# Attention on one core: value products in blocks of four steps, the reciprocal kept in PSUM, second-batch statistics later

## The reference

```python
h = _layernorm(x, axis=-1) * (1 + ca) + sa          # x: (2, 2048, 256)
q = _split_heads(x @ Wq + bq, 16)                   # 16 heads of 64
k = _split_heads(x @ Wk + bk, 16)
v = _split_heads(x @ Wv + bv, 16)
pattern = jnp.einsum('bhid,bhjd->bhij', k, q) * scale
prob = jax.nn.softmax(pattern, axis=-2)
out = jnp.einsum('bhis,bhid->bhsd', prob, v)
x = x + ga * (concat @ Wo + bo)
```

## Time and profile before

| | |
|---|---|
| median of 3 runs | 4973.08 us (4967.43 to 4975.9) |
| the profiled execution | 4973.04 us, its span 4971.3 us |
| mean granted clock of PE | 0.966 of 2.4 GHz |
| PE busy | 4594.8 us, 92% |
| DVE, POOL, ACT busy | 3502.5 us (70%), 2747.1 us (55%), 2208.0 us (44%) |

### The profile page before, as it was taken

How to read it: one execution, slowest core, us unless ns; L and a number is a source line. 1 busy time by engine, 2 the same in 40 slices (tenths; PEclk the granted TensorE clock), 3 DMA queues, 4 the chain that set the end, 5 groups by cost and what they waited for, 6 DMA issues and landing times.

```text
span 4971.3 us, 65114 instructions
## 1 busy us (share of the span) xinstructions
PE 4594.8 (92%) x21552; PEld 2807.0 (56%) x21552; DVE 3502.5 (70%) x4564; ACT 2208.0 (44%) x3535; POOL 2747.1 (55%) x1172
## 2 busy tenths in 40 slices
PE   6999999999999999999999999957989897999898
PEld 5555555555555555555555555425767675767576
DVE  5878778788788888887877878664656444655455
ACT  5434344444443444444444443424655343556442
POOL 2656566656565666566656655715666223666322
PEclk9999999999999999999999999978999998999898
DMA  2000000000000000000000000010000100000001
GB/s 64 1 5 1 5 6 1 6 5 2 6 1 5 5 1 6 5 2 6 1 5 6 1 6 1 2 55 1 1 1 1 36 1 17 1 1 1 0 1 34
DMA packets 56826, 37.55 MB, mean 8 GB/s; under 512 B 32572, under 2 KB 55056, under 8 KB 56464
## 3 DMA queue, kind: packets, MB, share of 16 engines
q1 hardware_dynamic: 56464, 33.02, 2.3%
HBM read 28.54 MB, written 4.19 MB: 7 GB/s over the span
## 4 chain that ended last, share of the span: by engine, by line
POOL 47%; issue 28%; PE 13%; DVE 7%; ACT 4%; POOLq 1%; DMA 0%; DVEq 0%; SPq 0%; ACTq 0%
POOL accp L709 36%; PE psum L1703 4%; POOL lp L731 4%; PE psum L1578 3%; POOL accp L705 3%; POOL rnorm L721 2%; POOL qk_u L726 2%; DVE ssq L1178 1%; ACT lp L894 1%; PE psum L1624 1%; ACT qk_sq L878 1%; PE psum L1716 1%; DVE qk_w L1190 1%; DVE lneg L1204 1%; PE psum L412 1%
## 5 line engine op out<-in xcount | busy, mean ns | idle before, releaser
L709 POOL TENSOR_TENSOR accp<-accp,prob 128x1024 f32<-128x1024 f32 x640 | 1636.8, 2558 | 744.4 <-ACT prob L848 707.2
L848 ACT ACTIVATE prob<-psum 128x1024 f32<-128x1024 f32 x1024 | 1040.1, 1024 | 1632.3 <-PE psum L1429 1505.8
L1076 DVE TENSOR_REDUCE mx<-psum 128x1 f32<-128x512 f32 x1984 | 1273.3, 683 | 419.9 <-PE psum L1400 380.5
L1440 PE MATMUL psum<-prob,vv 128*64 128x512 f32 x4096 | 997.3, 608 | 0.0
L1428 PE MATMUL psum<-qhh,klh 128*128 128x512 f32 x2048 | 840.7, 411 | 39.3 <-issue 20.4
L1429 PE MATMUL psum<-qlm,kh 65*128 65x512 f32 x2048 | 829.2, 405 | 0.0
L1400 PE MATMUL psum<-klh,qhh 128*128 128x512 f32 x1984 | 727.5, 426 | 56.6 <-DVE mx L1076 52.3
L1400 PEld LDWEIGHTS psum<-klh,qhh 128*128 128x128 f32 x1984 | 353.2, 192 | 467.8 <-DVE mx L1076 307.6
L1440 PEld LDWEIGHTS psum<-prob,vv 128*64 128x64 f32 x4096 | 249.6, 136 | 515.0 <-issue 369.8
L1428 PEld LDWEIGHTS psum<-qhh,klh 128*128 128x128 f32 x2048 | 398.7, 195 | 200.1 <-issue 86.2
L1429 PEld LDWEIGHTS psum<-qlm,kh 65*128 65x128 f32 x2048 | 398.7, 195 | 95.0 <-issue 7.6
(11 more groups left out here) (190 smaller groups left out, 6580.3 us busy)
## 6 DMA issues: line engine op xcount, KB each, us to landing
rot_l<-const_rot SPq DMA_DIRECT2D x2, 2048.0 KB, 8.7
out<-lpT SPq DMA_DIRECT2D x32, 128.0 KB, 1.8
wqkv_l<-L_ffn_wqkv SPq DMA_DIRECT2D x4, 768.0 KB, 9.8
w_l<-L_ffn_w SPq DMA_DIRECT2D x4, 682.0 KB
wqk<-L_attn_Wq SPq DMA_DIRECT2D x32, 64.0 KB, 2.2
wqk<-L_attn_Wk SPq DMA_DIRECT2D x32, 64.0 KB, 2.2
wv_p<-L_attn_Wv SPq DMA_DIRECT2D x16, 128.0 KB, 2.3
wo_p<-L_attn_Wo SPq DMA_DIRECT2D x16, 128.0 KB, 2.0
```

Of the source, the lines that this page charges most:

```text
L709: pool.tensor_tensor(acc_p[cp][:], first[:], prob[kt % PRING][:], ALU.add).then_inc(pool_sum, 1)
L848: act.activation(prob[t % PRING][:], psum[:, S_BANK + 2 * (t % 2):S_BANK + 2 * (t % 2) + 2, :].rearrange("p a b -> p (a b)"), ACT.Exp, sca ...
L1076: dve.tensor_reduce(mx4[:, j // CHUNKS, j % CHUNKS:j % CHUNKS + 1], ps, AX_X, ALU.max).then_inc(ring_free, 1)
L1440: mm = pe.matmul(psum[j * DH:(j + 1) * DH, O_BANK, :], vv[:, kt, s * DH:(s + 1) * DH], prob[t % PRING][:, j * T:(j + 1) * T], start=(kt == ...
```

## The change

Four edits:

- **Blocks of four.** `VALUES = 4`: PE's order is scores of four steps with some nine ring tiles spread between them, then the value products of four steps in one block. `PRING` is 8. The ring tiles are redistributed (`max_places`), and one order entry moves: at the head's end the block of steps 28 to 31 stands behind all four `proj_qk` items, where before steps 28 and 29 stood ahead of them.
- **Reciprocal in PSUM.** The reciprocal is written over the SUM's own ring place, and the two multiplications read it there. The place is released behind the multiplications; before it was released behind the reciprocal. Buffer `rcp` goes.
- **Second-batch statistics later.** ACT evicts the first hidden tiles first; means and squares are interleaved with the evictions of `vv` and with the reads of the input.
- **Buffers.** Three quarters of the second batch's input and a scratch tile lie in `prob[4:8]`; ACT's first exponential waits until POOL has normalised them (`h1_ok`).

```diff
-PRING = 4
+PRING = 8
...
-        GROUPS = STEPS // 2
-        SUM0_GROUP = (KT + 5) // 2
+        VALUES = 4
+        GROUPS = STEPS // VALUES
+        SUM0_GROUP = (KT + 5) // VALUES
+        OUT_GROUPS = 2
+        OUT_EACH = WO_ITEMS // OUT_GROUPS
+        TURN_EACH = 2
...
-            weight = [4] * (GROUPS - 1) + [0]
-            weight[0] = 1
-            weight[SUM0_GROUP + 1:SUM0_GROUP + 3] = [0, 2]
+            weight = [8] * (GROUPS - 1) + [4]
+            weight[0] = 6
+            weight[SUM0_GROUP + 1] = 4
...
-                if g + 1 < GROUPS:
-                    order += tiles[:cut0] + [("scores", 2 * g + 2)] + tiles[cut0:cut1] + [("scores", 2 * g + 3)] + tiles[cut1:]
-                else:
+                steps = range(VALUES * (g + 1) - 2, min(VALUES * (g + 2) - 2, STEPS))
+                n = len(steps)
+                for j, t in enumerate(steps):
+                    order.append(("scores", t))
+                    order += tiles[len(tiles) * j // n:len(tiles) * (j + 1) // n]
+                if g + 1 == GROUPS:
+                    if projects:
+                        order += [("proj_qk", i) for i in range(2)]
                     if maxima:
                         order.append(("turn", 0))
                     if projects:
-                        order += [("proj_qk", i) for i in range(QK_ITEMS)]
-                order += [("values", 2 * g), ("values", 2 * g + 1)]
+                        order += [("proj_qk", i) for i in range(2, QK_ITEMS)]
+                order += [("values", VALUES * g + j) for j in range(VALUES)]
...
-            next_statistics(0)
-            next_statistics(1)
             act.wait_ge(su_d, 3)
...
+                (next_squares if i % 2 else next_means)(i // 2)
+            next_means(2)
+            next_squares(2)
             act.wait_ge(gabo_ok, B)
-            for k in range(TWINS):
+            for k in range(2 * TWINS):
                 read_input(k)
...
+            next_means(3)
+            next_squares(3)
...
+            act.wait_ge(h1_ok, QUADS - 1)
...
-                dve.reciprocal(rcp[:], ps).then_inc(ring_free, 1)
-                dve.wait_ge(ring_free, OFF_RING + RING + rb + i + 1)
+                dve.reciprocal(ps, ps).then_inc(rcp_ok, 1)
+                dve.wait_ge(rcp_ok, G * CP + cp + 1)
...
-                                           o_raw[cp][rows, :], rcp[rows, :], ALU.mult)
-                op.then_inc(oT_ready, 1)
+                                           o_raw[cp][rows, :], ps[rows, :], ALU.mult)
+                op.then_inc(ring_free, 1)
+                dve.wait_ge(ring_free, OFF_RING + RING + rb + i + 1)
+                dve.sem_inc(oT_ready, 1)
```

More of the change, by code:

```diff
@@ L181, in adaln_block @@
         st_rs = sb("st_rs", [P, B, KT], at=att)
-        squares = [sb("squares", [P, 2, D], at=att), o_raw[0][:].rearrange("p (t d) -> p t d", d=D)]
+        squares = [prob[7][:, 0:2 * D].rearrange("p (t d) -> p t d", d=D), o_raw[0][:].rearrange("p (t d) -> p t d", d=D)]
         copies = o_raw[1][:].rearrange("p (t d) -> p t d", d=D)
@@ L189, in adaln_block @@
         x_quads = [[quad(t) for t in acc_p + acc_d],
-                   [x_tail[:, 4 * q:4 * q + 4, :] for q in range(3)] + [x_last[:]]]
+                   [quad(t) for t in prob[4:7]] + [x_last[:]]]
         h_quads = [[quad(t) for t in prob], [h_next[:, 4 * q:4 * q + 4, :] for q in range(QUADS)]]
@@ L292, in adaln_block @@
         PH_STORE = PH_L0 + 2 * LAYERS
-        GROUPS = STEPS // 2
-        SUM0_GROUP = (KT + 5) // 2
+        VALUES = 4
[4 more added lines that the diff above has]
+        TURN_EACH = 2
         def max_places(outs):
-            weight = [4] * (GROUPS - 1) + [0]
-            weight[0] = 1
-            weight[SUM0_GROUP + 1:SUM0_GROUP + 3] = [0, 2]
+            weight = [8] * (GROUPS - 1) + [4]
+            weight[0] = 6
+            weight[SUM0_GROUP + 1] = 4
             for g in outs:
-                weight[g] = 3
+                weight[g] = 6
             return [-(-RING_MAX * sum(weight[:g + 1]) // sum(weight)) for g in range(GROUPS)]
         FIRST, MIDDLE, BRIDGE, LAST = 0, 1, 2, 3
-        TURN_GROUP = 1 + WO_ITEMS // 2
+        TURN_GROUP = 1 + OUT_GROUPS
         def head_order(which, hh):
@@ L316, in head_order @@
             maxima, projects = not (last and hh), not last
-            outs = () if which == FIRST or hh else range(1, 1 + WO_ITEMS // 2)
-            turns = range(TURN_GROUP, TURN_GROUP + TWINS) if which == BRIDGE and hh == 0 else ()
+            outs = () if which == FIRST or hh else range(1, 1 + OUT_GROUPS)
+            turns = range(TURN_GROUP, TURN_GROUP + TWINS // TURN_EACH) if which == BRIDGE and hh == 0 else ()
             placed = max_places([*outs, *turns])
@@ L325, in head_order @@
                 if g in outs:
-                    tiles += [("out", 2 * (g - 1)), ("out", 2 * (g - 1) + 1)]
+                    tiles += [("out", OUT_EACH * (g - 1) + j) for j in range(OUT_EACH)]
                 if g in turns:
[L328 to L332, removed]
-                if g + 1 < GROUPS:
-                    order += tiles[:cut0] + [("scores", 2 * g + 2)] + tiles[cut0:cut1] + [("scores", 2 * g + 3)] + tiles[cut1:]
-                else:
+                    tiles += [("turn_h", TURN_EACH * (g - TURN_GROUP) + j) for j in range(TURN_EACH)]
+                steps = range(VALUES * (g + 1) - 2, min(VALUES * (g + 2) - 2, STEPS))
[6 more added lines that the diff above has]
+                        order += [("proj_qk", i) for i in range(2)]
                     if maxima:
@@ L780, in centred_squares, with next_means @@
                     act.activation(squares[b][:, i % 2, :], x_quads[b][q][:, t, :], ACT.Square, bias=st_neg[:, b, i:i + 1], accum_out=st_ssq[:, b, i:i + 1]).then_inc((sq_ok, sq1_ok)[b], 1)
-            def next_statistics(q):
+            def next_means(q):
                 if q == 0:
@@ L789, in next_statistics, with next_squares @@
                     act.activation(copies[:, i % 2, :], x_quads[1][q][:, t, :], ACT.Copy, scale=-1.0 / D, accum_out=st_neg[:, 1, i:i + 1]).then_inc(neg1_ok, 1)
+            def next_squares(q):
                 act.wait_ge(neg1_ok, 4 * (q + 1))
```

2 lines of the change are left out of this document (removed).

## The result

The changed kernel took 5036.32 us (median of 4 runs, 5032.78 to 5037.19) against 4970.26 us before (4 runs): ratio 1.0131, 95% interval 1.0114 to 1.0149. It is **slower by 66 us**, on the forecast's side and inside its range, 48 us above the predicted 4988. The profiled execution has a span of 5035.3 us at a mean granted clock of 0.953 of 2.4 GHz.

The account below looks back on a forecast made before the run. PE's own sequence was taken to bound the heads, so a change counts by what it removes or adds as waits. The terms -87 - 14 + 42 + 55 + 4 + 15 = +15 gave 4988 us, range 4935 to 5045.

Parts of the forecast that it names:

- Part 2, the start: At the start, moving ACT's statistics behind the evictions removes waits of PE and DVE: together -14 us.
- Part 3, the multiplication: In the heads, DVE's multiplication reading PSUM leaves contention with POOL and takes 0.69 us, bounds 0.69 and 2.04.
- contended rival: In the heads, the multiplication stays contended with POOL at 2.04 us: +84, 5072 us; chance 0.12.
- Part 4, the third max tile: Behind the middle SUM, PE waits 1.75 us for the ring place held until the multiplications end: +42 us.
- Part 5, the late add: At the SUM ending a pair's first head, PE waits 7.2 us for the add chain, 15 times: +55 us.
- hidden-add rival: At the SUM, POOL's chain ends before PE arrives, so the late add costs no wait: 4865 us; chance 0.05.
- Part 1, fewer blocks: In 31 heads, 16 value blocks become 8, saving 0.35 us for each of 248 blocks: -87 us.
- Part 6, the clock: Behind the longer waits at head boundaries, PE's clock falls low; 1 us added each: +15 us.
- rival in which the clock goes the other way: In the heads, denser blocks of four recover half the time lost to the low clock: 4943 us; chance 0.2.
- Part 5's last sentence: Behind a pair's second head, the values' projection covers the add chain; only 0.25 us remains each time: +4 us.
- the -60 of the old waits: At head boundaries, PE's old waits for DVE's last projection item and a ring place, 4.0 us 15 times, vanish.
- the -12 at the ring: Behind the middle SUM, DVE's backlog had cost PE some 0.4 us later; this was subtracted, 31 times.

Follow-up runs that it names:

- e6: The changed kernel with the reciprocal written to an SBUF buffer again and the ring place released behind it: 5201.02 us, ratio 1.0446.
- e3: The changed kernel with the group behind the middle SUM given weight 1, so one max tile stands there: 5011.66 us, ratio 1.0042.
- e7: The changed kernel with tile 12's add ahead of the projections in both heads and ring weights 3 (first group), 1 (behind the SUM), 5 (last): 4901.36 us, ratio 0.9845.
- e8: The kernel before, still in blocks of two, with the reciprocal in PSUM and the later second-batch statistics: 4871.79 us, ratio 0.9783.
- e1: The changed kernel with DVE's add of tile 12 ahead of the four projection items in both heads of a pair: 4954.51 us, ratio 0.9914.
- e9: The changed kernel with DVE's fourth tile 11 in place of 12 and the ring tiles spread in another way: 4942.5 us, ratio 0.9925.
- after_again: The changed kernel run once more, unaltered, against the kernel before: 5034.82 us, ratio 1.0114.
- e2: The changed kernel with DVE's add of tile 12 ahead of the projection items in the second head of a pair alone: 5033.67 us, ratio 1.0077.
- e12: The kernel before in blocks of two, with PSUM reciprocal, late statistics and the add of tile 12 behind the projections: 5073.38 us, ratio 1.0186.
- e10: The kernel before in blocks of two, with PSUM reciprocal, late statistics and DVE's fourth tile 11 in place of 12: 4870.88 us, ratio 0.9777.

## Why the prediction was right in direction and 48 us short

**Part 2, the start (-14):** measured -16.8.

**Part 3, the multiplication (0.69 us):** measured 0.686, never contended. The rule of the GPSIMD Engine Reference of the Trainium skill (Specifications), that POOL contends with VectorE instructions that have two SBUF inputs, agrees with both sides: one input in PSUM has one duration, and e6, back in SBUF, has 1565 ns and 157 us more. The trace before separates the cases: 23 of the 128 multiplications ran with POOL idle, and all took 683 to 690 ns; 101 had a POOL add beside them for over half of their time, with a median of 2522. In the change 81 of 128 had one, and none took over 693. The contended rival is out.

**Part 4, the third max tile (1.75 us, +42):** measured 1.53; 31 x (1.53 - 0.4) = +35. e3 removes it and gains 44, so with the low clock behind it this part was right to within a few us.

**Part 5, the late add (7.2 us, +55):** measured 6.97, with each step of the chain within 0.15 us of the walk. 15 x (6.97 + 0.45 - 4.0) = +51. The hidden-add rival is out.

**Part 1, fewer blocks (-87):** what the break costs was right, but it is not net. In the change a block behind a bunch of two max tiles has the break of before, one behind three has more. The timeline has one of each; the sum goes from the first tile of the bunch to the second record behind the block:

```profile
2038.05 0.64 PE L1409 MATMUL psum<-klh,qhh 128*128 128x512 f32 x2
2038.62 3.65 PE L1449 MATMUL psum<-prob,vv 128*64 128x512 f32 x16
2042.20 0.50 PE L1437 MATMUL psum<-qhh,klh 128*128 128x512 f32 x1
2042.54 0.40 PE L1438 MATMUL psum<-qlm,kh 65*128 65x512 f32 x1
...
2057.34 1.01 PE L1409 MATMUL psum<-klh,qhh 128*128 128x512 f32 x3
2058.28 3.65 PE L1449 MATMUL psum<-prob,vv 128*64 128x512 f32 x16
...
2062.20 0.40 PE L1438 MATMUL psum<-qlm,kh 65*128 65x512 f32 x1
```

Behind two tiles it is 4.49 us, where 3 x 0.23 + 8 x 0.43 = 4.13 would do: 0.36. Behind three it is 4.86, where 4.36 would do: 0.50. With 90 blocks behind three and 57 behind two in the heads the mean is 0.45, and the gain 31 x (16 x 0.35 - 8 x 0.45) = -62. e7 against e8 (both at a clock of 0.99) shows what comes back once the two large waits are gone. Adding up all 12,174 start-to-start spacings of PE's records by what stands on either side (each kind's sum, less 0.233 us for each spacing by which the two counts differ), the value blocks with their entries and the record behind them take 89 us less in blocks of four, as predicted. But spacings from a max tile to a max tile take 48 more, to scores behind a max tile 18 more, between scores 22 more, and those at the SUMs, output tiles and projections some 19 more: +107, net +18. **In e7 half as many blocks bring no net gain.** In the change itself much less comes back. Spacings 0.15 to 1.0 us over the full-clock one of their kind, outside the low stretches, add up to 35 us in 101 places, against 19 in 71 before, 66 in 146 in e1, and 107 in 308 in e7 (e8: 13 in 43). So the -62 holds for the change, and the loss comes up as the waits go. My reading is that the 7-us waits gave DVE the time to catch up; and that the bunches of two and three tiles in a ring of three are what it falls behind with is argued from these spacings and from e9's waits. No run changed the bunches with all else equal.

**Part 6, the clock (+15), the first step that was mis-sized.** "I add 1 us each" was about right behind the waits, but it left out the loop starts. After the terms above and the loop starts the balance is -62 - 17 + 35 + 51 + 17 = +24, and 66 were measured: **42 us** remain. The count of the stretched spacings gives the same: 88 less 47 is +41. By what stands ahead of each low stretch, 40 us lie behind waits at the SUM, 15 behind ring waits and 31 behind the 11 loop starts (in after_again 36, 15, and 27 at the loop starts and the waits at the scores right behind them); before, 39 lay behind waits for the ring or at the scores, 3 at the SUM and 2 behind a loop start. So behind the waits the low level costs 12 us more, about what the prediction put down; the other 30 lie behind loop starts, which it had not counted. The rule that was weighed there, of TensorE: Matmul & The Clock Gate of the Trainium skill (What's actually happening), that the throttled state is the default and activity releases it, agrees with that; what was missed is a place where PE sits still. The rival in which the clock goes the other way is out.

**Part 5's last sentence (second heads, "only the 0.25 remain, +4"), the second step, and the one whose mechanism failed.** PE does arrive at the SUM with POOL done, as written. But POOL is done only 0.33 us ahead, and the first scores behind the loop's branch then start 1.6 us later on average, 11 x 1.6 = +17. The walk asked when the matmul needs its data; it left out PE's sequencer, which must pass the SUM's wait before it can start the branch of 3.3 to 4.1 us. The branch records above show this in each of the 11 places, and e1, e2 and e12 move the branch with the add: it starts 1.5 us ahead of the SUM in e1 and e2, and 0.10 behind it in e12. Why a taken branch takes that long is not known from these runs.

So the clock is +27 off, the loop starts +13 and part 1 +25, the start, part 4 and part 5 together -14: 51, which is the step from the +15 of the sum to the +66 measured.

**How much of it was luck.** Taken apart by runs and not by waits, the same change splits otherwise. The PSUM reciprocal and the late statistics gave -108 (e8), where the sum has -86 for them (-14, the -60 of the old waits and the -12 at the ring). Blocks of four gave +31 (e7 against e8), forecast -87. The held ring place gave +34 (e1 against e7), forecast +54, and the late add +108 (e1), forecast +134 with the clock. The largest miss, 118 us on the blocks, is partly made up by the three others. The range had some luck too: half way from 4988 to the contended 5072 is 5030, not the 5045 that was written, and 5036 lies between; the most likely band, slower by 10 to 60 us, was missed by 6.

The kernel that the experiments point to is e8 (or e10, the same within the intervals): 4872 us, 2.2% below before and, by the ratios, 3.4% below the change.

## What to carry to other kernels

When an add, or any small link of a chain over several engines, moves behind a batch of other work on its engine, walk the whole chain to the engine that sets the pace; here 1.2 us of DVE work put 7 us of wait on PE, and the time at half clock and a late loop start made it 108. Walk it for the sequencer too: a wait ahead of a loop's end can be met in time for the matmul and still hold up the branch. An operand in PSUM that takes a DVE instruction out of contention with POOL was worth more (94 us) than saving half of PE's switches between tile shapes, which larger blocks had to pay for in a ring of three places. Try such parts one by one: two of the three gained here, and the third hid it. What a part is worth depends on the others: the late add costs 108 us in blocks of four and 200 in blocks of two (e12 against e8).

## What was not expected of the hardware

- A semaphore wait that is satisfied a third of a microsecond before PE gets there costs nothing at the waiting instruction, and yet the first matmul behind the next loop start comes 4.09 us after the SUM in place of 2.19; with 1.48 us of real wait it is 4.32. The taken branch itself takes 3.27 to 4.12 us of PE's sequencer in the traces counted here, and it is hidden only as far as matmuls are queued ahead of it.
- The low clock costs less than its share: 194 us more of it in e12 took 48 us; part of it lies over waits.
- Both parts of the break can be read apart: 0.33 in place of 0.23 us from the last max tile into a value block, 0.34 between the first two records behind it (2042.20 to 2042.54), and 0.14 from the last value product to the first of them (3.58 from 2038.62 to 2042.20, less 8 x 0.43).
